# Attention: another order on a shared PSUM bank, and bulk transfers in parts that wait for a group's maxima

## The chip, the cores and the metric

One NeuronCore of a Trainium2 chip runs the whole kernel in one launch. Its engines work from their own instruction streams and meet at semaphores: TensorE (PE; its weight loads are shown as PEld), VectorE (DVE), ScalarE (ACT), GpSimd (POOL) and SyncE (SP), which here only issues DMA transfers. All transfers run on the core's 16 DMA engines; SyncE's show as queue q1, ScalarE's as q10. The metric is the device time of the kernel in microseconds (us).

## The reference

x has 8 sequences of 512 tokens with 128 channels. Four layers add to it, each on a layer norm of x: an RWKV recurrence, a mixture of experts, the attention of this case, and the same mixture of experts again. The attention, cut to what matters (16 heads of 8 channels):

```
q, k, v   = x @ Wq, x @ Wk, x @ Wv                    # split into heads
amp(t)    = softplus(t) / sqrt(mean(softplus(t)**2, over the head) + 1e-6)
q_phi     = pi * tanh(x @ Wqp);   k_phi = pi * tanh(x @ Wkp)
scores    = (q.k + lam * (amp(q) cos(q_phi) . amp(k) cos(k_phi)
                        + amp(q) sin(q_phi) . amp(k) sin(k_phi))) / sqrt(8)
out       = softmax(causal(scores)) @ v               # over the keys, 512
x         = x + out @ Wo
```

So a query and a key of a head are vectors of 24 numbers, and the score is one dot product. The softmax is taken with the row's maximum subtracted.

## The kernel before, in words

`attention_stage` (L704) works on 8 **blocks** b, one sequence each. A block has two **units** q of 8 heads, and a unit two halves of 4 heads. I call a half a **quarter** of the block: quarter g = 0 to 3 is unit g // 2, half g % 2. A quarter is ten **slots**; the block's slots are numbered 0 to 39 here. All engines walk the same slots in program order, each at its own pace.

What TensorE does in a slot: `scores` (L1009) computes a piece of the scores of the current unit into one of three regions (`attn_ps_q`, `attn_ps_v`), which ScalarE exponentiates (L1205 to L1210); `scores_for_maximum` (L961, L966, L970) computes scores of the *next* unit the other way round into three further regions (`attn_ps_p`, `attn_ps_t`), of which VectorE takes row maxima (L1458); and `between` does what the slot has besides. `weigh_values` (L1034) multiplies the exponentials of the quarter before with the values, in slots 3 and 5 of a quarter.

**Maxima.** For each quarter the maxima are transposed into the shared bank by TensorE (`turn_maxima`, L996), copied negated by ScalarE (`take_maxima`, L1225), the remainder is split off by VectorE (`split_maxima`, L1463, with the semaphore step at L1466), and ScalarE sends both parts by two transfers of 8 KB (`send_maxima`, L1230) into two rows of the stack of queries, so that the matmul subtracts them. TensorE may not start the quarter's first `scores` before they have landed (`neg_max_landed`). M0a, M0b, M1a, M1b name these uses for unit 0 or 1 and half a or b. M1a is turned in the first half of quarter 1 for the quarter that follows, M0b in quarter 0, M1b in quarter 2, and M0a of the next block in quarter 3.

**The shared bank.** `attn_ps_f` is one PSUM bank that eight kinds of work use in turn: M0a to M1b as above; A0 and A1, the means of the squared softplus of queries and of keys of block b + 2 (`mean`, L942; ScalarE's `log_of_mean`, L1180, frees the bank); E0 and E1, the outputs of a unit turned (`turn_output`, L1044; VectorE's `normalise`, L1476 and L1478, frees it); FT, the normalised rows turned (L1050; ScalarE's L1235 frees it); FW, the projection (`project`, L1056; VectorE adds it to x at L1486). The list `order` gives the sequence of uses; every user waits on `f_free` until all uses before its own are through.

**Features.** The amplitudes and circles of block b + 2 are worked out inside block b: `features` says in which slot which step runs, on ScalarE (`size`, `exponential_of_size`, `log_of_sum`, `squares`, `log_of_mean`, `inverse`, `high`) and on VectorE (`softplus`, `amplitude`, `scale_circle`, `low`). Side 0 is the queries, side 1 the keys; `high` and `low` (L1195, L1447) split each of three parts into two numbers for the matmul. ScalarE's `high` of part 1 or 2 waits for VectorE's `scale_circle` of the same.

**SyncE.** Its stream per block: `keep` (L846) writes a side's six parts to DRAM (1536 KB), `refill` (L852 to L856, four transfers, 1152 KB) reads the stack of one quarter of block b + 1 back in the layout for the matmul, once the last scores of that quarter of block b are done, and `fetch` (L842) reads the values of block b + 3 (1792 KB). SyncE issues in program order: what waits holds back all behind it.

## Time and profile before

| | us |
|---|---|
| median of 3 runs (lowest, highest) | 1274.72 (1273.44, 1281.04) |
| the profiled execution's own time | 1278.36 |
| its span | 1276.6 |
| mean granted clock of TensorE | 0.923 |
| attention loop, first to last `scores` | 611.1 to 1033.7 |

The quarter starts in the trace (the first L1009 matmul of each) are, for blocks 1 to 6: 671.0, 683.7, 699.5, 716.0; 728.4, 742.1, 755.5, 771.3; 785.7, 799.6, 813.0, 828.8; 841.7, 855.1, 868.5, 884.3; 896.6, 908.1, 920.8, 936.8; 950.2, 962.8, 974.9, 986.6. A row of the view by windows gives for each engine the busy time and the number of instructions inside, then the granted TensorE clock as a share of 2.4 GHz (0.50 is 1.2 GHz), the busy share of the 16 DMA engines and what they moved. In the view of waits a line says which instruction of an engine stood idle and which instruction or landing ended it. In the timeline the brackets hold the idle time just before. An operation in float32 takes TensorE two instructions or more, which the timeline merges (x2, x4).

### The profile page before, as it was taken

Reading aid. Unit: us, or ns where it says so; the run is one execution under the profiler, and the core shown is the slowest. Engines: PE = TensorE matmul, PEld = TensorE weight load, DVE = VectorE, ACT = ScalarE, POOL = GpSimd, SP = SyncE. Lnnn points to the kernel's source line nnn. Section 1 sums busy time; section 2 is a strip of 40 time slices with the busy share of each in tenths; the row PEclk is TensorE's granted clock in tenths of the full one; section 3 lists DMA queues with packets and bytes.
Section 4 is the critical chain, followed back from the end, with each engine's and each line's share of the span. In section 5 each row is a group of like instructions: output and inputs, shape, how many; then the busy total and the mean of one; then the engine's idle time right before and its main releaser. Section 6 shows DMA issues by size and latency. Waiting matters only on the chain. (4 is left out here: it accounts for less than half of the span.)

```text
span 1276.6 us, 16117 instructions
## 1 busy us (share of the span) xinstructions
PE 1093.0 (86%) x5200; PEld 649.7 (51%) x5200; DVE 906.5 (71%) x1927; ACT 656.6 (51%) x1204; POOL 267.2 (21%) x300
## 2 busy tenths in 40 slices
PE   3888889975999999776788888888888969999996
PEld 1223223324676667434455555555556636666774
DVE  2778998976877876874676666667766618787775
ACT  1234444425555555584556565665755546555553
POOL 1445565630000000220212111121212210000000
PEclk9789998977999999886698898989989989999999
DMA  5000000001232121439776767586755312323311
GB/s 192 0 1 1 0 0 1 0 1 46 88 119 81 67 71 63 102 129 259 248 183 141 204 165 193 137 205 169 170 141 136 61 67 67 134 67 99 101 67 66
DMA packets 45502, 129.04 MB, mean 101 GB/s; under 512 B 6512, under 2 KB 8560, under 8 KB 38768
## 3 DMA queue, kind: packets, MB, share of 16 engines
q1 hardware_dynamic: 43376, 127.53, 35.4%
q8 instruction: 41, 0.67, 0.2%
q10 hardware_dynamic: 2048, 0.53, 0.2%
q14 instruction: 37, 0.30, 0.1%
HBM read 88.72 MB, written 36.70 MB: 98 GB/s over the span
## 5 line engine op out<-in xcount | busy, mean ns | idle before, releaser
L1458 DVE TENSOR_REDUCE attn_maxima<-attn_ps_p 128x1 f32<-128x512 f32 (+3 forms) x235 | 146.0, 637 | 106.0 <-PE attn_ps_p L966 88.2
L1377 POOL TENSOR_SCALAR_AFFINE_SELECT attn_probs<-attn_probs 128x512 f32<-128x512 f32 x128 | 84.7, 696 | 321.8 <-ACT attn_probs L1210 321.8
L1835 ACT ACTIVATE moe_hidden<-moe_ps_h 128x512 f32<-128x512 f32 x128 | 76.3, 596 | 146.0 <-PE moe_ps_y L1773 144.3
L961 PE MATMUL attn_ps_p<-attn_stack 96*128 96x384 f32 (+3 forms) x341 | 121.3, 399 | 11.0 <-DVE attn_maxima L1458 10.0
L1957 DVE TENSOR_TENSOR moe_gated<-moe_ps_y,moe_gate_all 128x512 f32<-128x512 f32 x106 | 73.1, 690 | 75.2 <-issue 46.8
L1009 PE MATMUL attn_ps_q<-attn_stack 128*128 128x128 f32 (+3 forms) x343 | 108.8, 381 | 12.4 <-DMA attn_stack<-attn_neg_max 10.9
L1755 PE MATMUL moe_ps_h<-moe_x_high,moe_w_high 128*128 128x512 f32 x256 | 107.4, 420 | 0.0
L1458 DVE TENSOR_REDUCE attn_maxima<-attn_ps_t 128x1 f32<-128x384 f32 (+3 forms) x117 | 74.4, 636 | 44.1 <-PE attn_ps_t L966 41.8
L1757 PE MATMUL moe_ps_h<-moe_x_high,moe_w_low 128*128 128x512 f32 x256 | 102.8, 402 | 0.0
L1756 PE MATMUL moe_ps_h<-moe_x_low,moe_w_high 128*128 128x512 f32 x256 | 102.4, 400 | 0.0
L1771 PE MATMUL moe_ps_y<-moe_hidden_high,moe_w_low 128*128 128x512 f32 x128 | 101.0, 789 | 0.0
L587 POOL TENSOR_TENSOR rwkv_rs<-rwkv_recept,rwkv_state 128x512 f32<-128x512 f32 x64 | 75.9, 1186 | 104.9 <-DVE rwkv_state L668 102.3
L668 DVE TENSOR_TENSOR_SCAN rwkv_state<-rwkv_decay,rwkv_kv 128x512 f32<-128x512 f32 x64 | 91.5, 1429 | 3.2
L1988 DVE TENSOR_TENSOR moe_hidden_low<-moe_hidden,moe_hidden_high 128x512 fp32r<-128x512 f32 x128 | 87.6, 685 | 6.3 <-ACT moe_hidden_high L1836 6.2
L1034 PE MATMUL attn_ps_o<-attn_probs,attn_v_ones 128*32 128x512 f32 (+3 forms) x1024 | 87.2, 461 | 1.7 <-POOL attn_probs L1377 1.7
L224 POOL TENSOR_TENSOR moe_rstd<-moe_var_eps,minus_half 128x4 f32<-128x4 f32 x16 | 16.1, 1009 | 313.0 <-DVE moe_var_eps L208 313.0
L961 PEld LDWEIGHTS attn_ps_p<-attn_stack 96*128 96x128 f32 x341 | 68.8, 215 | 22.4 <-DVE attn_maxima L1458 17.5
L1009 PEld LDWEIGHTS attn_ps_q<-attn_stack 128*128 128x128 f32 x343 | 60.6, 201 | 36.0 <-issue 16.9
L1838 ACT ACTIVATE moe_hidden<-moe_ps_h 128x512 f32<-128x512 f32 x128 | 77.1, 602 | 0.4 <-PE moe_ps_h L1757 0.4
L1966 DVE TENSOR_TENSOR moe_total<-moe_total,moe_gated 128x512 f32<-128x512 f32 x112 | 76.4, 682 | 0.3
L1836 ACT ACTIVATE moe_hidden_high<-moe_ps_h 128x512 fp32r<-128x512 f32 x128 | 75.7, 591 | 0.0
L1207 ACT ACTIVATE attn_probs<-attn_ps_q 128x512 f32<-128x512 f32 x86 | 51.7, 601 | 32.8 <-PE attn_ps_q L1009 29.9
(256 smaller groups left out, 2426.8 us busy)
## 6 DMA issues: line engine op xcount, KB each, us to landing
moe_gate_all<-moe_gates SPq DMA_DIRECT2D x128, 256.0 KB, 4.9
attn_kept<-attn_parts SPq DMA_DIRECT2D x16, 1536.0 KB, 7.9
attn_stack<-attn_kept SPq DMA_DIRECT2D x64, 384.0 KB
attn_stack<-attn_kept SPq DMA_DIRECT2D x64, 192.0 KB
attn_value<-attn_values SPq DMA_DIRECT2D x5, 1792.0 KB, 12.3
attn_values<-attn_early SPq DMA_DIRECT2D x2, 1792.0 KB, 5.7
attn_values<-attn_probs SPq DMA_DIRECT2D x2, 1792.0 KB, 21.9
experts_in_w<-in_w SPq DMA_DIRECT2D x2, 1024.0 KB, 11.3
```

The costliest lines, as they stand in the source:

```text
L668: nc.vector.tensor_tensor_scan(state[:, n, 1:T + 1], decay[:, s, :], kv[:, n % 2, :], 0.0, ALU.mult, ALU.add).then_inc(state_ready, 1)
L961: return mm(tiles(m)[:, i, :], stack[0][q][0:ROWS, h + i, t * P:(t + 1) * P], stack[1][q][0:ROWS, h + i, 0:(t + 1) * P], **flags)
L1009: return mm(ps_h[n % 3][:, at:at + width], stack[1][q][:, h, j * P:(j + 1) * P], stack[0][q][:, h, j * P:T], start=True, stop=True)
L1034: last = mm(ps_o[32 * hh:32 * hh + 32, j * P:T], v_ones[:, b % 2, j, 4 * g + hh, :], probs[:, g % 2, hh, at:at + width], start=(g % 2 == 0 ...
L1377: nc.gpsimd.affine_select(out=tile, in_=tile, compare_op=ALU.is_ge, fill=0.0, base=0, pattern=[[0, 4], [1, P]], channel_multiplier=-1).the ...
L1458: nc.vector.tensor_reduce(maxima[:, u % 2, h:h + heads, t], tiles, AX_X, ALU.max).then_inc(g_free, 1)
L1755: mm(out[:], w1_high[:, cols], x_high[:, c % 3, :], start=True, stop=False)
L1756: mm(out[:], w1_high[:, cols], x_low[:, c % 3, :], start=False, stop=False)
L1757: mm(out[:], w1_low[:, cols], x_high[:, c % 3, :], start=False, stop=True).then_inc(up_done, 1)
L1771: mm(ps_y[s][:], w2_low[:, first], hidden_high[:, s, :], start=False, stop=False)
L1838: fn(hidden[:, s, T:], ps_h[s][1][:], ACT.Gelu).then_inc(gelu_done, 1)
L1988: tt(hidden_low[:, s, :], hidden[:, s, 0:T], hidden_high[:, s, :].bitcast(F32), ALU.subtract).then_inc(low_ready, 1)
```

## The change

Three things are changed, all inside `attention_stage`; the arithmetic is the same.

1. **The order on the shared bank.** A0 of block b + 2 moves from behind FT and FW to between M0b and E1: TensorE does it in slot 5 instead of slot 20. E0 goes from slot 28 to 29, FW from slot 17 to 18, the splits of maxima from the fifth to the fourth slot of a quarter, the normalisation of E0 from slot 29 to 30, the residual add from 18 to 19.
2. **The features' slots.** The first steps of side 0 (`size` to `softplus`) run in the last eight slots of the block before (for block 2, ahead of the loop), the others of side 0 about 15 slots earlier, and each `high` at least three slots behind its `scale_circle`.
3. **SyncE.** Each `keep` becomes two of 768 KB (the high parts, the low parts), `fetch` becomes one of 768 and one of 1024 KB. `sent(u, half)` waits until the maxima of that quarter have landed; one stands ahead of each later part. In a block: refill 0, fetch part 1, *wait for M1a*, fetch part 2, refill 1, keep of side 0 high, *wait for M1b*, keep low, refill 2, *wait for M0a*, keep of side 1 high, refill 3, keep low, *wait for M0b*.

```diff
-    STACK = 4 * 16
+    STACK, KEPT = 4 * 16, 2 * 16
...
         order += [("M0b", b)]
+        order += [("A0", b + 2)] if b + 2 < NB else []
         order += [("E1", b - 1)] if b else []
         order += [("M1a", b)]
         order += [("FT", b - 1), ("FW", b - 1)] if b else []
-        order += [("A0", b + 2)] if b + 2 < NB else []
         order += [("M1b", b)]
...
-            def fetch(b):
-                sp.wait_ge(stored[b], 16)
-                for s in range(2):
-                    sp.wait_ge(low_ready[s], 3 * (b - 1))
-                sp.wait_ge(v_ready, b - 1)
-                sp.dma_start(value[b % 2][:].rearrange("p n t -> p (n t)"), value_kept[b]).then_inc(loaded[b % 2], 16)
...
+            def fetch(b, part):
+                if part == 0:
+                    sp.wait_ge(stored[b], 16)
+                    for s in range(2):
+                        sp.wait_ge(low_ready[s], 3 * (b - 1))
+                    sp.wait_ge(v_ready, b - 1)
+                at = slice(0, 3 * T) if part == 0 else slice(3 * T, FULL)
+                sp.dma_start(value[b % 2][:].rearrange("p n t -> p (n t)")[:, at],
+                             value_kept[b][:, at]).then_inc(loaded[b % 2], 16)
+
+            def keep(b, s, part):
+                if part == 0:
+                    sp.wait_ge(high_ready[s], 3 * b + 3)
+                else:
+                    sp.wait_ge(low_ready[s], 3 * b + 3)
+                at = slice(3 * part, 3 * part + 3)
+                sp.dma_start(scratch[b][s].rearrange("n d h t -> (d h) n t")[:, at, :],
+                             parts[s][:, at, :].bitcast(F32)).then_inc(kept[s], 16)
+
+            def sent(u, half):
+                sp.wait_ge(neg_max_landed[half], (u + 1) * 32)
...
+            for b in range(LAST):
+                keep(b + 1, 1, 1)
+                sent(2 * b, 1)
+                refill(b, 0, 0)
                 if b + 3 < NB:
-                    fetch(b + 3)
-                if b < LAST:
-                    refill(b, 1, 0)
+                    fetch(b + 3, 0)
+                sent(2 * b + 1, 0)
+                if b + 3 < NB:
+                    fetch(b + 3, 1)
+                refill(b, 0, 1)
                 if b + 2 < NB:
-                    keep(b + 2, 0)
-                if b < LAST:
-                    refill(b, 1, 1)
+                    keep(b + 2, 0, 0)
+                sent(2 * b + 1, 1)
+                if b + 2 < NB:
+                    keep(b + 2, 0, 1)
+                refill(b, 1, 0)
+                sent(2 * b + 2, 0)
+                if b + 2 < NB:
+                    keep(b + 2, 1, 0)
+                refill(b, 1, 1)
...
-                if g == 2 and at == 0 and b + 2 < NB:
+                if g == 0 and at == 5 and b + 2 < NB:
                     mean("A0", b + 2)
...
-                if at == 8 and g == 2:
+                if at == 9 and g == 2:
                     turn_output("E0", b)
```

A few lines of ScalarE's `features` and `between`:

```diff
+                if k == 6:
+                    log_of_mean(b, 0)
...
                 if k == 14:
-                    high(b, 0, 0)
+                    high(b, 0, 1)
...
-                if k == 21:
-                    log_of_mean(b, 0)
...
-                if k == 25:
-                    high(b, 0, 1)
...
                     features(b + 2, 20 * q + k)
+                if b + 3 < NB:
+                    features(b + 3, 20 * q + k - 40)
```

And of VectorE's:

```diff
+                if k == 11:
+                    scale_circle(b, 0, 1)
...
-                if k == 25:
-                    scale_circle(b, 0, 1)
...
-                if at == 4:
+                if at == 3:
...
-                if at == 9 and g == 2:
+                if at == 0 and g == 3:
                     normalise("E0", b)
```

How the instructions stand in three places. The changed kernel's line numbers are 11 to 25 higher for the same function. **TensorE in slots 5 to 7 of a block**, before and now:

```order
L1034 MATMUL attn_ps_o<-attn_probs,attn_v_ones 32x256 x4
L1034 MATMUL attn_ps_o<-attn_probs,attn_v_ones 32x128 x4
L1009 MATMUL attn_ps_v<-attn_stack 128x384
L1009 MATMUL attn_ps_v<-attn_stack 128x128
L961 MATMUL attn_ps_t<-attn_stack 128x512
```

```order
L1055 MATMUL attn_ps_o<-attn_probs,attn_v_ones 32x256 x4
L1055 MATMUL attn_ps_o<-attn_probs,attn_v_ones 32x128 x4
L963 MATMUL attn_ps_f<-attn_soft,attention_in_mean_head 128x512
L1030 MATMUL attn_ps_v<-attn_stack 128x384
L1030 MATMUL attn_ps_v<-attn_stack 128x128
L982 MATMUL attn_ps_t<-attn_stack 128x512
```

A0's matmul (L963) has come in behind the weighing of slot 5, three slots ahead of E1. **VectorE at the end of quarter 0 and in quarter 1**, before and now:

```order
L1478 TENSOR_TENSOR attn_xn<-attn_ps_f,attention_in_w 128x4x64
L1427 SCALAR_TENSOR_TENSOR attn_amp<-attn_value,attn_soft 128x512
L1458 TENSOR_REDUCE attn_maxima<-attn_ps_p 128x4
L1458 TENSOR_REDUCE attn_maxima<-attn_ps_t 128x2
L1458 TENSOR_REDUCE attn_maxima<-attn_ps_p 128x2
L1458 TENSOR_REDUCE attn_maxima<-attn_ps_p 128x1
L1427 SCALAR_TENSOR_TENSOR attn_amp<-attn_value,attn_soft 128x512
L1458 TENSOR_REDUCE attn_maxima<-attn_ps_t 128x1
L1463 SCALAR_TENSOR_TENSOR attn_neg_max<-attn_ps_f,attn_neg_max 16x128
```

```order
L1503 TENSOR_TENSOR attn_xn<-attn_ps_f,attention_in_w 128x4x64
L1483 TENSOR_REDUCE attn_maxima<-attn_ps_p 128x4
L1458 SCALAR_TENSOR_TENSOR attn_amp<-attn_amp,attention_in_columns,attn_soft 128x512
L1483 TENSOR_REDUCE attn_maxima<-attn_ps_t 128x2
L1468 TENSOR_TENSOR attn_value<-attn_value,attn_amp 128x512
L1483 TENSOR_REDUCE attn_maxima<-attn_ps_p 128x2
L1468 TENSOR_TENSOR attn_value<-attn_value,attn_amp 128x512
L1483 TENSOR_REDUCE attn_maxima<-attn_ps_p 128x1
L1488 SCALAR_TENSOR_TENSOR attn_neg_max<-attn_ps_f,attn_neg_max 16x128
L1472 TENSOR_TENSOR attn_parts<-attn_value,attn_parts 128x512
L1483 TENSOR_REDUCE attn_maxima<-attn_ps_t 128x1
```

The two softplus have left; the amplitude (L1458 of the changed kernel), both scalings (L1468) and the low part (L1472) of the queries stand between the reductions of quarter 1's first slots, and the split has one reduction fewer ahead of it. **SyncE from the fetch on**, before and now:

```order
L842 DMA attn_value<-attn_values 128x3584 [waits attn_low_ready1,attn_v_ready,attn_low_ready0,attn_stored3]
L852 DMA attn_stack<-attn_kept 48x2048 [waits attn_h_done]
L853 DMA attn_stack<-attn_kept 24x2048
L855 DMA attn_stack<-attn_kept 24x2048
L856 DMA attn_stack<-attn_kept 48x2048
L846 DMA attn_kept<-attn_parts 128x6x512 [waits attn_low_ready0]
```

```order
L844 DMA attn_value<-attn_values 128x1536 [waits attn_low_ready1,attn_v_ready,attn_low_ready0,attn_stored3]
L844 DMA attn_value<-attn_values 128x2048 [waits attn_neg_max_landed0]
L863 DMA attn_stack<-attn_kept 48x2048 [waits attn_h_done]
L864 DMA attn_stack<-attn_kept 24x2048
L866 DMA attn_stack<-attn_kept 24x2048
L867 DMA attn_stack<-attn_kept 48x2048
L853 DMA attn_kept<-attn_parts 128x3x512 [waits attn_high_ready0]
L853 DMA attn_kept<-attn_parts 128x3x512 [waits attn_low_ready0,attn_neg_max_landed1]
```

The fetch now stands one refill earlier in the block (behind refill 0 instead of refill 1), and its second part and the keep's second part wait for a landing of maxima.

## Rows read from the trace of the kernel before

**Rows 1.** Windows (blocks 4, 6, loop): window, length, busy per engine, PEclk, DMA share, GB/s

```profile
841.70:896.60 54.90, 47.32 (x336) 30.36 (x336) 36.76 (x67) 32.94 (x65) 11.12 (x18) 0.95 0.70 177
950.20:996.50 46.30, 42.54 (x335) 27.57 (x335) 29.91 (x55) 25.92 (x50) 10.71 (x18) 1.00 0.63 138
611.10:1033.70 422.60, 363.64 (x2573) 232.45 (x2573) 275.49 (x494) 250.21 (x486) 91.91 (x146) 0.93 0.63 159
```

**Rows 2.** Windows of single quarters; in order of the text: blocks 1, 4, 5

```profile
683.70:699.50 15.80, 14.37 (x91) 9.66 (x91) 7.52 (x14) 8.81 (x18) 3.12 (x6) 0.78 0.39 77
841.70:855.10 13.40, 12.87 (x81) 8.71 (x82) 6.46 (x11) 6.80 (x14) 2.48 (x4) 0.78 0.73 192
855.10:868.50 13.40, 11.66 (x93) 7.66 (x93) 9.03 (x17) 10.26 (x22) 3.53 (x6) 1.00 0.48 91
868.50:884.30 15.80, 12.40 (x89) 7.56 (x89) 9.87 (x18) 8.13 (x17) 2.39 (x4) 1.00 0.71 192
884.30:896.60 12.30, 10.39 (x81) 6.44 (x80) 11.40 (x22) 7.74 (x16) 2.72 (x4) 1.00 0.88 236
896.60:908.10 11.50, 10.50 (x82) 6.74 (x82) 7.51 (x14) 7.75 (x16) 2.85 (x4) 1.00 0.86 232
936.80:950.20 13.40, 12.78 (x81) 8.31 (x78) 10.90 (x20) 6.52 (x14) 2.84 (x4) 0.76 0.77 208
```

**Rows 3.** Waits of TensorE, 625 to 1045: us in total, times, longest

```profile
PE attn_ps_q L1009 <- DMA attn_stack<-attn_neg_max: 9.7, 6, 2.9
PE attn_ps_f L1044 <- ACT attn_soft L1180: 7.5, 6, 1.3
PE attn_ps_f L942 <- DVEq L1466: 5.6, 6, 0.9
PE attn_ps_f L1044 <- ACT attn_o_rows L1218: 4.6, 9, 0.7
PE attn_ps_f L1056 <- ACT attention_in_w L1235: 4.3, 8, 0.7
PE attn_ps_f L1050 <- DVEq L1466: 4.3, 7, 0.8
PE attn_ps_v L1009 <- DMA attn_stack<-attn_neg_max: 3.4, 3, 1.8
PE attn_ps_f L942 <- DVE x_rows L1486: 1.8, 5, 0.4
```

**Rows 4.** Timeline, block 4's third quarter: start, us, engine, what, idle before it

```profile
877.88 1.46 ACTq L1230 DMA_DIRECT2D attn_stack<-attn_neg_max  x2
...
878.06 1.10 PE L942 MATMUL attn_ps_f<-attn_soft,attention_in_mean_head 128*128 128x512 f32 x2 [0.93 <-DVEq L1466]
...
880.96 0.63 ACT L1195 ACTIVATE attn_parts<-attn_value 128x512 fp32r<-128x512 f32 x1 [4.17 <-DVE attn_value L1443]
...
882.45 0.69 ACT L1180 ACTIVATE attn_soft<-attn_ps_f,attention_in_columns 128x512 f32<-128x512 f32 x1
...
883.29 0.63 PE L1044 MATMUL attn_ps_f<-identity,attn_o_rows 128*128 128x128 f32 x4 [1.26 <-ACT attn_soft L1180]
```

**Rows 5.** Tile attn_neg_max, issue to landing: sent in 862.5:867, 877.5:882.5, 778.5:786

```profile
DMA to landing us min/median/max: 2.2/2.3/2.3
...
DMA to landing us min/median/max: 3.2/3.3/3.4
...
DMA to landing us min/median/max: 3.9/4.8/5.6
```

**Rows 6.** Windows around the maxima sent at 877.88; columns as in rows 1

```profile
877.00:880.00 3.00, 2.07 (x16) 1.30 (x10) 1.08 (x4) 0.00 (x0) 0.00 (x0) 1.00 0.92 388
880.00:881.00 1.00, 1.00 (x7) 0.60 (x5) 1.00 (x3) 0.04 (x1) 0.00 (x0) 1.00 0.11 29
```

**Rows 7.** VectorE by form, 671 to 950: busy us, mean ns, idle before

```profile
L1447 DVE TENSOR_TENSOR attn_parts<-attn_value,attn_parts 128x512 fp32r<-128x512 f32 x30 | 23.4, 779 | 0.0
L1443 DVE TENSOR_TENSOR attn_value<-attn_value,attn_amp 128x512 f32<-128x512 f32 x20 | 13.6, 681 | 0.0
```

More of the change, by code:

```diff
@@ L825, in wait_loaded @@
         def wait_loaded(engine, b):
-            engine.wait_ge(loaded[b % 2], (b - 1) // 2 * 16)
+            engine.wait_ge(loaded[b % 2], (b - 1) // 2 * 32)
         block = ctx.enter_context(nc.Block())
@@ L870, in _ @@
             store(4)
-            keep(0, 0)
-            keep(0, 1)
+            for s in range(2):
+                for part in range(2):
+                    keep(0, s, part)
             sp.wait_ge(zeroed, 32)
             for s in range(2):
-                sp.wait_ge(kept[s], 16)
+                sp.wait_ge(kept[s], KEPT)
             stack_heads(0, 0, 0)
@@ L883, in _ @@
             store(7)
-            keep(1, 0)
-            for b in range(NB):
-                if b < LAST:
-                    keep(b + 1, 1)
-                    refill(b, 0, 0)
-                    refill(b, 0, 1)
-                if b + 3 < NB:
-                    fetch(b + 3)
-                if b < LAST:
-                    refill(b, 1, 0)
-                if b + 2 < NB:
-                    keep(b + 2, 0)
-                if b < LAST:
-                    refill(b, 1, 1)
+            keep(1, 0, 0)
+            keep(1, 0, 1)
+            keep(1, 1, 0)
+            for b in range(LAST):
+                keep(b + 1, 1, 1)
+                sent(2 * b, 1)
+                refill(b, 0, 0)
+                if b + 3 < NB:
+                    fetch(b + 3, 0)
[3 more added lines that the diff above has]
+                refill(b, 0, 1)
+                if b + 2 < NB:
+                    keep(b + 2, 0, 0)
[7 more added lines that the diff above has]
+                refill(b, 1, 1)
         @block.tensor
@@ L1237, in features @@
             def features(b, k):
-                if k == 4:
+                if k == -7:
                     size(b, 0)
-                if k == 5:
+                if k == -6:
                     exponential_of_size(b, 0)
+                if k == -4:
+                    log_of_sum(b, 0)
+                if k == 0:
+                    squares(b, 0)
+                if k == 6:
+                    log_of_mean(b, 0)
                 if k == 7:
-                    log_of_sum(b, 0)
+                    inverse(b, 0)
                 if k == 8:
@@ L1267, in features @@
                     inverse(b, 1)
[L1268 to L1270 removed]
+                if k == 34:
                     high(b, 1, 1)
[L1272 removed]
+                if k == 36:
                     high(b, 1, 2)
@@ L1347, in _ @@
                 inverse(1, s)
+            for k in range(-8, 0):
+                features(2, k)
             for b in (5, 6):
@@ L1488, in features @@
             def features(b, k):
[L1489 removed]
+                if k == -3:
                     softplus(b, 0)
+                if k == 10:
+                    amplitude(b, 0)
+                if k == 11:
+                    scale_circle(b, 0, 1)
+                if k == 12:
+                    scale_circle(b, 0, 2)
                 if k == 13:
+                    low(b, 0, 0)
+                if k == 15:
                     softplus(b, 1)
                 if k == 16:
[L1494 to L1495 removed]
+                    low(b, 0, 1)
+                if k == 18:
+                    low(b, 0, 2)
+                if k == 22:
                     low(b, 1, 0)
[L1497 to L1504 removed]
+                if k == 30:
+                    amplitude(b, 1)
                 if k == 31:
[L1506 removed]
+                    scale_circle(b, 1, 1)
                 if k == 32:
[L1508 to L1511 removed]
                     scale_circle(b, 1, 2)
[L1513 removed]
+                if k == 36:
                     low(b, 1, 1)
[L1515 removed]
+                if k == 38:
                     low(b, 1, 2)
@@ L1529, in between @@
                         split_maxima("M0a", b + 1, 2 * b + 2)
-                if g == 1 and at == 8 and b:
+                if g == 1 and at == 9 and b:
                     add_output(b - 1)
@@ L1537, in between @@
                     features(b + 2, 20 * q + k)
+                if b + 3 < NB:
+                    features(b + 3, 20 * q + k - 40)
                 if b == 0 and q == 0 and k in (2, 3):
@@ L1582, in _ @@
                 scale_circle(1, s, 2)
+            for k in range(-8, 0):
+                features(2, k)
             for b in range(NB):
```

41 lines of the change are left out of this document (9 added, 32 removed).

## The prediction, made before the changed kernel was run

> **What bounds the kernel now.** I read the views in this order: the stretches of the attention loop, the waits of TensorE inside it, the timeline around the largest of them, and then the landings of the small transfers against the load of the DMA engines. The loop is the only place the diff touches; it takes 422.6 us of the 1276.6 us span [rows 1].
>
> TensorE is the bound, but not at its peak. A block with features in it (blocks 0 to 5) takes 54.9 us with TensorE busy for 47.3; block 6, which has the same scores and outputs but no features, takes 46.3 at a full clock [rows 1]. The quarters of one block are very unequal [rows 2]: in block 4 they are 13.4, 13.4, 15.8 and 12.3 us. Two things stretch them. The third quarter (868.5) is busy for only 12.4 of its 15.8 us. And the first quarter of block 4 (841.7; those of blocks 2 and 3 are like it) is busy for 12.9 us where block 5's (896.6), the same work at a granted clock of 1.00, is busy for 10.5: the granted clock averages 0.78 in it, a mixture of 2.4 and 1.2 GHz.
>
> The waits of TensorE name the causes [rows 3]. From 625 us on it waits 9.7 + 3.4 = 13.1 us for the landing of a quarter's negated maxima, and 7.5 + 5.6 + 4.6 + 4.3 + 4.3 = 26.3 us for the shared bank (attn_ps_f). The timeline of block 4's third quarter [rows 4] shows what is behind the largest: ScalarE waits 4.17 us for the scaled circle it must copy (`high` in slot 25, `scale_circle` in the same slot on VectorE), so its logarithm of A1 comes at 882.45, and TensorE, at slot 28, waits 1.26 us for it before E0. Before A1 it had waited 0.93 us for VectorE's split of M1b.
>
> The landings: sent onto quiet DMA engines the maxima need 2.3 us in the median; sent onto busy ones 3.3 and 4.8 us [rows 5]. The 3.3 are of the pair sent at 877.9: the engines are 0.92 busy with 388 GB/s of bulk until 880, and 0.11 in the microsecond after [rows 6].
>
> **The change, part by part.** No arithmetic is added. TensorE, ScalarE and VectorE run the same instructions in another order; SP issues two keeps and one fetch per block more.
>
> 1. *Maxima against bulk.* Today a refill and, behind it, a whole keep (1536 KB) or fetch (1792 KB) are issued at once at the end of a quarter, in three quarters of four, and are still draining when the maxima are sent six or more slots in. The change leaves behind each refill at most one part of 768 KB; the next part goes out when the maxima have landed. In block 4's third quarter the bulk drains at 880, 11.5 us in; a fetch of 1792 KB at 388 GB/s [rows 6] is 4.6 us of that, a part of 768 KB would be 2.0, so the engines would be free 2.6 us earlier, about 9 us in. The maxima leave 9.4 us into it, at 877.88 [rows 4]. Bounds: nothing of the 13.1 us, or all. Two things stop short of all: the fourth bulk burst (refill, half a keep, and the half keep issued late in the quarter before) still ends near the send of M0b, and block 0's is behind the start-up stores. I take 9 us.
>
> 2. *The shared bank.* A0 leaves the crowded stretch after FW for slot 5, between M0b and E1. E0 moves from slot 28 to 29, FW from 17 to 18, all splits one slot earlier, and ScalarE's copies of the circle come three slots or more behind their scaling. A slot is 1.34 us (13.4 us over ten). E0 behind A1 (7.5 us): the 4.17 us wait of ScalarE is gone, E0 is a slot later; 6.5 go. A1 behind the split (5.6): 0.93 each time, less than the slot won; 5 go. FT behind the split (4.3): 3.5 go. FW behind ScalarE's copy (4.3): 4 go. E1 behind the copied output (4.6, with E0's own): here the change adds. ScalarE copies the output in slot 6 and then takes A0's logarithm (0.69 us, [rows 4]) before E1 in slot 8 may write; TensorE has the mean's own matmul, 1.10 us [rows 4], more to do meanwhile; A0 has a wait for a split too. I add 2 us over six blocks. A0's old wait behind the residual add was 1.8; 1.5 go. Sum: 6.5 + 5 + 3.5 + 4 + 1.5 - 2 = 18.5 us. Bounds: nothing, and 26.3 + 1.8 = 28.
>
> 3. *The clock.* Five quarters are at 0.75 to 0.78; three stand in rows 2. Against their like at 1.00 these are busy for 2.4 us more (12.87, against 10.50), 2.7 more (14.37 against 11.66) and 2.4 more (12.78 against 10.39); with the two others like the first, some 12.5 us. Four begin with a landing wait, the fifth follows a wait before E0 like the one in rows 4. Block 6, with a landing wait of its own, stays at 1.00 throughout [rows 1]: the trace shows a coincidence, not the cause. Bounds 0 and 13; I take 9.
>
> 4. *What is late next.* VectorE. Its second quarter is 9.03 us busy of 13.4; its fourth 11.40 of 12.3 [rows 2]. The change puts into the second quarter an amplitude and two scalings (0.68 each, by the scaling) and two low parts (0.78 each) more than it had [rows 7], 3.6 us: 12.6 busy, where the quarter, 13.4 less its two bank waits of 0.8 and 0.5 [rows 3], should last 12.1. The fourth loses one low part and gains a softplus and the normalisation of E0, about 0.7 us: 12.1 in a quarter that without the landing wait behind it should be 11.4. The first and third are light, and TensorE may be three score tiles ahead, so most of this is carried over; not covered it would cost 0.5 + 0.7 = 1.2 us a block. I take that whole, 7 us for six blocks. Before the loop ScalarE has three more activations for block 2, which were inside it, each about as long as the 0.69 us one of [rows 4]: 2 us at the start if nothing hides them; I add 1.5. SP's three more issues stand beside everything. Its new waits hold back the refills behind them, but a refill may go only at the end of a quarter, when these maxima have landed anyway (TensorE itself waits for them there).
>
> Sum: 9 + 18.5 + 9 - 8.5 = 28 us. The profiled execution took 1278.4 us and would take 1250; it lies 3.7 above the median of the runs, 1274.7, and in their range. From the median: **1247 us**.
>
> **A rule that speaks against part 1.** In the trace the loaded maxima land about when the bulk ahead is through: the pair sent at 877.9 lands a microsecond later than a quiet one, at about 881.5, when the engines have just emptied [rows 5, 6]. The Trainium skill, page "DMA: Bandwidth & Descriptors", section "Queues, rings and completion order", says that each engine takes turns between the queues that have work, a packet at a time; then a small transfer on ScalarE's own queue would wait for one packet of bulk, however much stands behind it, and holding parts back would win little. What the trace shows of the loaded landings (4.8 against 2.3 us) speaks for a longer wait than one packet's, but it holds few cases.
>
> **Rivals.**
> - *Landings as late as before* (0.15): lateness comes from any bulk in flight, not from its amount. Parts 1 and 3 give nothing: 18.5 - 8.5 = 10 us, 1265. By the Trainium skill's rule above it would end here. For it: the engines are 0.86 and 0.88 busy over the quarters at 896.6 and 884.3 [rows 2], and a shorter quarter packs the same bytes tighter (0.70 of 54.9 us in block 4 is 38 us of bulk, 0.80 of a block of 48). Against it: the landing follows the drain in rows 6.
> - *VectorE becomes the bound* (0.12): quarters two and four last what VectorE has to do plus a hand-over of one operation each, 0.7 us: 13.3 and 12.8. That is 1.4 us a block more than I took: 1255.
> - *All of it works* (0.10): 13 + 26 + 13 us less 7: 1230.
> - *Slower* (0.04): the new place of A0 becomes what slot 20 to 28 was. ScalarE has in slots 5 to 9 the issue of two transfers, the output, the logarithm, the inverse, a size and a high part beside five exponentials. If it falls over three slots behind there, E1 stalls for the 1.26 + 0.93 us that E0 and A1 stall today, M1a is sent late and its landing costs up to 2.9 us, and the slower clock another 2.7: 7.8 us a block, 47 in six, against the forecast's gain of 28: 1294. It decides once E1's wait passes about 1 us in every block.
> - *No effect* (0.02): the waits only change their names, 1273.
> - The forecast (0.57) spans 1237 to 1257.
>
> **Range and chances.** 1232 to 1265 takes in the forecast, VectorE's bound and half of the first rival; out are about 0.07 below and 0.12 above. One per cent, about what a measurement of this kernel tells from none, is 12.7 us, so faster is below 1262: the forecast, the good case, VectorE's, and a third of the first rival, 0.84. Within 1%: 0.12. Slower: 0.04.
>
> **What the new profile would show.** Part 1: landings near 2.5 us in all quarters, TensorE's wait for them under 4 us in all. Part 2: the third quarters near 12 us, no wait of ScalarE for the scaling, E1's wait under 1 us. Part 3: granted clock 1.00 in most quarters from block 1 on. Part 4: VectorE busy over 11.5 us in the second and fourth quarters, TensorE's waits for reductions up by some 5 us. The whole loop near 394 us. I am wrong if landings stay at 4 us, if the first quarter takes over the stall of the third, or if the second quarter grows over 13.4 us.

## The result, and the profile after

The changed kernel takes 1257.51 us in the median of four runs (1256.41 to 1258.44), beside runs of the kernel before with a median of 1275.9: a ratio of 0.984, 95% interval 0.981 to 0.987. Forecast were 1247 in a range of 1232 to 1265, so the sign and the range hold, and about 10 us of the gain of 28 are missing. One disturbed run of 1980 us, of R7 below, is left out of its ratio.

The whole gain is in the attention loop, 422.6 us before [rows 1]. Windows of the changed kernel, columns as in rows 1: the loop, then the four quarters of block 4.

```profile
613.20:1015.60 402.40, 361.22 (x2575) 233.66 (x2573) 283.48 (x496) 252.59 (x488) 93.90 (x146) 0.93 0.70 167
...
831.90:846.30 14.40, 13.07 (x85) 8.09 (x85) 8.54 (x16) 7.86 (x16) 2.68 (x4) 0.88 0.78 194
846.30:858.00 11.70, 11.13 (x91) 7.63 (x91) 10.85 (x20) 9.12 (x19) 4.00 (x6) 1.00 0.77 172
858.00:871.80 13.80, 11.59 (x85) 7.25 (x85) 10.10 (x17) 8.05 (x16) 4.02 (x6) 1.00 0.84 220
871.80:885.20 13.40, 13.02 (x78) 8.38 (x79) 8.60 (x16) 7.81 (x16) 1.22 (x3) 0.75 0.71 153
```

The loop is 20.2 us shorter, the span 19.9. The second and third quarters have lost 1.7 and 2.0 us against those at 855.1 and 868.5 [rows 2], but the third does not reach the 12 that I forecast, and the first and fourth have each grown by about 1 us. TensorE is busy for 2.4 us less than before, at the same mean clock. The loss is seen in its waits, of the changed kernel from 625 to 1030 (us in total, times, longest):

```profile
PE attn_ps_q L1030 <- DMA attn_stack<-attn_neg_max: 14.5, 12, 2.9
PE attn_ps_p L982 <- DVE attn_maxima L1483: 6.0, 12, 0.8
PE attn_ps_v L1030 <- DMA attn_stack<-attn_neg_max: 5.8, 5, 1.5
...
PE attn_ps_t L982 <- DVE attn_maxima L1483: 4.2, 7, 0.8
PE attn_ps_v L1030 <- DVE attn_maxima L1483: 2.1, 1, 2.1
...
PE attn_ps_f L1017 <- DVE attn_xn L1503: 1.2, 4, 0.3
PE attn_ps_f L1017 <- DVE x_rows L1511: 1.1, 1, 1.1
PE attn_ps_f L1071 <- DVE attn_xn L1503: 0.9, 1, 0.9
PE attn_ps_f L1065 <- ACT attn_o_rows L1239: 0.7, 1, 0.7
PE attn_ps_f L1077 <- ACT attention_in_w L1256: 0.7, 1, 0.7
```

Those for the shared bank (attn_ps_f) are down to 4.6 us, where the six of [rows 3] alone were 28.1. Those for the landing of the maxima, which the parts were to shorten, are up from 13.1 us [rows 3] to 20.3. The landings themselves are slower. Tile attn_neg_max, issue to landing, sends from 640 to 1000, first of the kernel before, then of the changed one:

```profile
DMA to landing us min/median/max: 1.8/2.9/5.6
```

```profile
DMA to landing us min/median/max: 1.8/4.3/7.4
```

The timeline of the changed kernel around one of the late ones, at the start of block 3's fourth quarter, shows how (start, duration, engine, what, idle before it). SPq is SyncE's issue, ACTq ScalarE's:

```profile
811.50 1.16 ACTq L1251 DMA_DIRECT2D attn_stack<-attn_neg_max  x2
...
819.49 0.38 SPq L853 DMA_DIRECT2D attn_kept<-attn_parts  x1
...
819.52 0.50 PE L1030 MATMUL attn_ps_q<-attn_stack 128*128 128x512 f32 x1 [2.93 <-DMA attn_stack<-attn_neg_max]
...
819.91 0.48 SPq L863 DMA_DIRECT2D attn_stack<-attn_kept  x1
```

The pair sent at 811.50 lands after 7.1 us in the median, and TensorE has waited 2.93 us for it. Just before that matmul the keep that `sent` held back goes out, 0.42 us ahead of the refill of the new quarter. Nothing was moved out of the way of the next maxima: the part that should have gone out late in the old quarter goes out first in the new one. The amounts agree: around the start of block 3's third quarter SyncE issues the fetch's second part, a refill and half a keep (1024 + 1152 + 768 KB), ahead of the same maxima for which the kernel before had a refill and a whole fetch (1152 + 1792 KB), 2944 KB both times. SyncE's waits in the changed kernel, 625 to 1016, put a size to it:

```profile
SPq L853 <- DMA attn_stack<-attn_neg_max: 80.3, 12, 12.7
...
SPq L844 <- DMA attn_stack<-attn_neg_max: 40.5, 5, 11.0
```

That is 121 us in which it stood before a keep or a fetch until maxima had landed, 7 us each time, half a quarter.

### The profile page after: what moved, and what is told of

The parts are those of the page before. It is cut to its first block and busy times, and to the rows that moved or that the text cites. A ratio compares the mean times of both kernels' runs of the same rounds, so it can differ in the third digit from the quotient of the medians.

```text
span 1256.7 us, 16161 instructions
## 1 busy us (share of the span) xinstructions
PE 1094.3 (87%) x5200; PEld 654.1 (52%) x5200; DVE 913.6 (73%) x1927; ACT 658.0 (52%) x1204; POOL 269.2 (21%) x300
## 3 DMA queue, kind: packets, MB, share of 16 engines
q1 hardware_dynamic: 44352, 127.53, 37.1%
q10 hardware_dynamic: 2048, 0.53, 0.2%
## 5 line engine op out<-in xcount | busy, mean ns | idle before, releaser
L982 PEld LDWEIGHTS attn_ps_p<-attn_stack 96*128 96x128 f32 x341 | 68.8, 215 | 20.3 <-DVE attn_maxima L1483 13.3
```

The costliest lines, as they stand in the source:

```text
L982: return mm(tiles(m)[:, i, :], stack[0][q][0:ROWS, h + i, t * P:(t + 1) * P], stack[1][q][0:ROWS, h + i, 0:(t + 1) * P], **flags)
```

## The experiments

The runs are R0 to R10 and R12. In R1 and R2 the bank's order and the features stay or go together; R9 takes the one-slot moves alone. Each ratio is to runs of the kernel before on the same chip: R1 to R4 ran together, so did R0, R5, R6 and R7, so did R8, R9 and R10.

**R1, the order alone**: the changed order and features, the whole keeps and fetches of before at their old places, no `sent`.

```diff
-                keep(b + 1, 1, 1)
-                sent(2 * b, 1)
                 refill(b, 0, 0)
-                if b + 3 < NB:
-                    fetch(b + 3, 0)
...
+                    fetch(b + 3)
+                refill(b, 1, 0)
+                if b + 2 < NB:
+                    keep(b + 2, 0)
```

> The changed order on the shared bank and of the features, with SyncE's transfers as before: whole keeps and fetches, no wait for a landing. Theory S (the order is the whole gain, SyncE's part gives nothing because its waits end only at the quarter's end, where the held part then starts together with the next refill): 1254 to 1260 us, landing waits of TensorE 15 to 25 us as in the changed kernel. Rival P (the held parts do shield the maxima, and without them the waits would be longer still, since a shorter quarter packs the bulk tighter): 1263 to 1272, landing waits over 28 us.

**R2, SyncE's part alone**: the order and features of before, SyncE as changed.

```diff
-                if g == 0 and at == 5 and b + 2 < NB:
+                if g == 2 and at == 0 and b + 2 < NB:
                     mean("A0", b + 2)
...
-                if at == 9 and g == 2:
+                if at == 8 and g == 2:
                     turn_output("E0", b)
```

> The order before, with SyncE's parts and waits of the change. Theory S: 1272 to 1279 us, no change, landing waits still 10 to 15 us. Rival P: 1260 to 1268, landing waits under 6 us.

**R3, parts without waits**: the changed kernel with all four calls of `sent` taken out.

```diff
-                sent(2 * b + 1, 0)
                 if b + 3 < NB:
                     fetch(b + 3, 1)
```

> The changed kernel without SyncE's waits for landed maxima; the parts stay split and in their order. Theory S: within 3 us of the changed kernel's 1257.5, since the waits end where the next refill is due anyway. Rival P: 1262 or more, landing waits over 26 us (20 in the changed kernel).

**R4, nothing behind a refill**: every part is put behind the wait for a landing.

```diff
-                keep(b + 1, 1, 1)
                 sent(2 * b, 1)
+                keep(b + 1, 1, 1)
                 refill(b, 0, 0)
-                if b + 3 < NB:
-                    fetch(b + 3, 0)
                 sent(2 * b + 1, 0)
                 if b + 3 < NB:
+                    fetch(b + 3, 0)
                     fetch(b + 3, 1)
```

> The changed kernel with all keep and fetch parts moved behind the landing of their quarter's maxima, so that nothing but the refill stands between a quarter's start and its maxima. Theory D (a landing is late by the bulk still in the queue when it is sent, so the amount ahead decides): landing waits down from 20 to under 10 us, 1240 to 1250 us. Rival R (any bulk in flight delays it alike, a packet at a time): landing waits 15 to 20, 1255 to 1260. Rival L (the deferred parts start at the quarter's end all the same and meet the next refill): 1255 or more, landings still 5 us and more.

| | median us | ratio (95%) | loop us | waits for landings |
|---|---|---|---|---|
| R1 order alone | 1250.16 | 0.978 (0.974 to 0.982) | 402.4 | 16.7 |
| R2 SyncE alone | 1307.03 | 1.022 (1.018 to 1.027) | 450.3 | 32.3 |
| R3 parts, no waits | 1245.18 | 0.972 (0.969 to 0.976) | 394.3 | 15.8 |
| R4 all behind landings | 1272.23 | 0.994 (0.991 to 0.996) | 420.5 | 35.7 |

(The last column sums the two rows in which `scores` waits for attn_neg_max, of one profiled execution each; R0 below, the changed kernel again, has 23.2 where the first execution has 20.3.) The order and the features carry the whole gain. On SyncE's side the waits cost: with them 0.984, without them 0.972, and the more is put behind them, the worse. Of what I expected, rival P failed in each. Theory S, which put SyncE's part at nothing, failed too: R1 came out 4 us below its range, R2 28 us above it, and R3 is 1.2% faster than the changed kernel where S allowed 3 us. R4's time is rival L's. R1's profiled execution was its slowest (1264.75, where its lowest is 1247.65), so its loop overstates it; by the medians the order alone is also better than the order with the change's SyncE, though the two intervals just overlap. Whether parts without waits are better than none stays open: the intervals of R1 and R3 overlap.

**R0, the changed kernel once more**, beside the next three.

> The changed kernel itself, so that the runs beside it can be set against it on one chip: ratio 0.981 to 0.988 to the kernel before.

It repeats: 1259.57, ratio 0.984 (0.981 to 0.988).

**R5, the wait ends at the split**: `sent` waits for VectorE's split of the same maxima instead of their landing.

```diff
             def sent(u, half):
-                sp.wait_ge(neg_max_landed[half], (u + 1) * 32)
+                sp.wait_ge(neg_low, 2 * u + half + 1)
```

> The changed kernel with each of SyncE's waits ending when VectorE has split the maxima, so just before ScalarE sends them, instead of when they have landed. Theory C (a wait for the landing carries the held part over the quarter's end, ahead of the next refill, and so makes the next landing late in its turn): the held parts now go in the quarter they belong to, landing waits down from 20 to 10 to 15 us, ratio 0.970 to 0.976, as without waits or better. Rival H (what costs is any wait of SyncE at all, since it holds its queue up): ratio 0.980 to 0.988, as the changed kernel.

Measured 1242.0, ratio 0.970 (0.965 to 0.975), loop 389.1, landing waits 12.6: theory C's numbers. Holding parts back costs nothing that shows beside R3; holding them until the landing does. Timeline of R5 around the same quarter's start, block 3's fourth:

```profile
798.16 0.38 SPq L853 DMA_DIRECT2D attn_kept<-attn_parts  x1
798.17 1.16 ACTq L1251 DMA_DIRECT2D attn_stack<-attn_neg_max  x2
...
802.26 0.32 SPq L863 DMA_DIRECT2D attn_stack<-attn_kept  x1
...
803.58 0.51 PE L1030 MATMUL attn_ps_q<-attn_stack 128*128 128x512 f32 x1 [0.34 <-DMA attn_stack<-attn_neg_max]
```

The keep leaves with the maxima, 4 us before the refill, not in front of it, and TensorE waits 0.34 us where it waited 2.93.

**R6, all parts behind the split**: R4's places with R5's wait.

> All keep and fetch parts behind the split of their quarter's maxima, so that only the refill is ahead of a send. Theory D (bulk that stands in the queue when the maxima are sent delays them, bulk issued afterwards doesn't): landing waits under 8 us, ratio 0.960 to 0.970. Rival R (any bulk in flight delays them alike, also what comes behind): landing waits 15 us and more, ratio 0.972 to 0.985.

Measured 1245.41, ratio 0.973 (0.970 to 0.977), loop 384.5, landing waits 15.4, where the same places with the wait for the landing gave 0.994 and 35.7 (R4). These are rival R's numbers, but the run did not put the bulk behind the maxima, as the rows show. Two sends of R6 stand next to each other, one beside bulk and one in the clear. Its timeline, then issue to landing of the two pairs, then windows around them:

```profile
799.44 0.92 SPq L853 DMA_DIRECT2D attn_kept<-attn_parts  x2
799.45 1.16 ACTq L1249 DMA_DIRECT2D attn_stack<-attn_neg_max  x2
...
805.59 0.51 PE L1028 MATMUL attn_ps_q<-attn_stack 128*128 128x512 f32 x1 [1.07 <-DMA attn_stack<-attn_neg_max]
...
812.30 0.51 ACTq L1249 DMA_DIRECT2D attn_stack<-attn_neg_max  x1
```

```profile
DMA to landing us min/median/max: 4.7/5.1/5.6
...
DMA to landing us min/median/max: 1.8/1.8/1.9
```

```profile
797.00:799.40 2.40, 2.40 (x27) 1.15 (x23) 1.29 (x3) 0.98 (x2) 0.00 (x0) 1.00 0.81 133
800.00:803.00 3.00, 3.00 (x15) 1.94 (x16) 1.57 (x4) 1.73 (x4) 0.00 (x0) 1.00 0.92 326
803.00:806.00 3.00, 1.93 (x13) 1.24 (x13) 2.15 (x4) 1.90 (x4) 1.03 (x2) 1.00 1.13 327
811.50:814.50 3.00, 3.00 (x29) 1.96 (x28) 2.30 (x5) 2.85 (x6) 0.00 (x0) 1.00 0.04 8
```

The first pair needs 3.3 us more than the one in the clear. It was not ahead of the bulk. SyncE and ScalarE wait for the same split; the first part's issue starts 0.005 us before the send, here and in all 17 such pairs of the loop, the second part's 0.12 us before the second transfer's, and until 799.40 the engines were 0.81 busy with the refill.

**R7, nearly no bulk**: R3 with the keeps (from block 2) and the fetches cut to 16 columns, and refills that read the stack of block 1. It bounds what landings and their traffic cost.

```diff
-                at = slice(0, 3 * T) if part == 0 else slice(3 * T, FULL)
+                at = slice(0, 16) if part == 0 else slice(3 * T, 3 * T + 16)
...
-                stack_heads(b + 1, q, half)
+                stack_heads(1, q, half)
```

> Without SyncE's waits, and with the keeps from block 2 on and the fetches cut to 16 columns of each part; the refills stay whole and read block 1's stack. It leaves out work: the attention of later blocks is not the reference's. It prices the keeps' and fetches' contention. Theory D and C both: landing waits under 5 us, VectorE's tiles the only large wait left, ratio 0.955 to 0.965. If the slower clock follows the landing waits, the loop's time at half clock falls from 58 us to under 35; if it has other causes it stays over 45 and the ratio is 0.962 to 0.972.

Measured 1228.06, ratio 0.960 (0.955 to 0.964). The loop of R7, as a window, and its landings (sends from 620 to 980):

```profile
608.00:977.90 369.90, 344.20 (x2573) 223.02 (x2573) 283.46 (x495) 251.25 (x487) 95.09 (x146) 0.97 0.55 107
```

```profile
DMA to landing us min/median/max: 1.8/2.1/4.4
```

The waits for landings are under 1 us in all, and reductions are the only large wait left, as expected. Against R3 the loop loses 24.4 us, of which 12.2 are TensorE's busy time: the granted clock goes from 0.94 there (0.93 in the changed kernel) to 0.97, and the time at half clock from 58 us in the changed kernel to about 21.

**R8, the old order with parts and no waits**: R2 without `sent`.

> The order before, with SyncE's parts but without its waits for landings. Theory C (the waits do the harm, the split as such none): within 1% of the kernel before, ratio 0.990 to 1.005, where the same with waits was 1.022. Rival K (more and smaller transfers harm by themselves, or the old order cannot bear the parts' places, since a keep part that waits for a late low part holds up the refill behind it): ratio 1.012 or more.

Measured 1308.57, ratio 1.023 (1.019 to 1.027): the same as R2 and rival K's number. Here I was wrong: I had put R2's loss down to the waits, and they add nothing. The timeline of R8, from the start of a quarter (843.1) to the start of the next, and SyncE's largest waits, 625 to 1060:

```profile
843.89 5.36 SPq L853 DMA_DIRECT2D attn_kept<-attn_parts  x2
...
849.29 0.48 SPq L860 DMA_DIRECT2D attn_stack<-attn_kept  x1
...
854.18 1.15 ACTq L1244 DMA_DIRECT2D attn_stack<-attn_neg_max  x2
...
861.39 0.80 PE L1023 MATMUL attn_ps_q<-attn_stack 128*128 128x512 f32 x1 [3.92 <-DMA attn_stack<-attn_neg_max]
```

```profile
SPq L853 <- ACT attn_parts L1209: 125.6, 12, 17.1
...
SPq L860 <- PE attn_ps_q L1023: 56.6, 8, 11.4
...
SPq L853 <- DVE attn_parts L1461: 20.1, 6, 4.6
```

Both parts of the queries' keep now stand ahead of this refill. The first waits for ScalarE's last `high` (slot 29 in the old features) until 843.89, which costs little, as the refill may go only from 843.1 on. The second waits 4.6 us more for VectorE's last `low` (slot 31, in the next quarter). So the refill goes out at 849.29, about 5 us after it could, and is still under way when the maxima leave at 854.18. The pair needs 6.4 us, and TensorE waits 3.92. R3 has the same places with the new order and the features 15 slots earlier, and 0.972. So R2 and R8 price this clash with the old features; they say nothing of what the parts alone would do.

**R9, five moves of one slot**: the kernel before, with FW and E0 on TensorE a slot later, the splits a slot earlier, and the residual add and E0's normalisation a slot later. This is the whole edit beside the one line `if at == 4` that becomes `if at == 3`:

```diff
-                if g == 1 and at == 7 and b:
+                if g == 1 and at == 8 and b:
                     project(b - 1)
-                if at == 8 and g == 2:
+                if at == 9 and g == 2:
                     turn_output("E0", b)
...
-                if g == 1 and at == 8 and b:
+                if g == 1 and at == 9 and b:
                     add_output(b - 1)
-                if at == 9 and g == 2:
+                if at == 0 and g == 3:
                     normalise("E0", b)
```

> The kernel before with the one-slot moves alone: splits a slot earlier, E0 and its normalisation, FW and the residual add a slot later; A0, the features and SyncE as before. Theory M (the bank's waits are mostly a slot short each): bank waits of TensorE down from 29 to under 16 us, ratio 0.985 to 0.992. Rival F (the features' places cause them, by ScalarE's 4 us wait for the scaled circle): bank waits still over 20 us, ratio 0.992 to 1.003; A0, now one slot closer behind the residual add, waits longer.

Measured 1242.24, ratio 0.972 (0.969 to 0.976), loop 386.6: with A0, the features and SyncE left alone, it is faster than the changed kernel. It is no slower than R1 either (0.978, the intervals just overlap), which has these moves and those of A0 and the features: nothing shows that the latter two gain anything. Of R9: the loop and the four quarters of a block as windows, TensorE's waits for the bank from 625 to 1020, and the wait of ScalarE that I had blamed:

```profile
610.10:996.70 386.60, 348.66 (x2573) 225.96 (x2573) 276.15 (x494) 248.32 (x486) 91.75 (x146) 0.96 0.70 174
817.70:830.50 12.80, 10.50 (x86) 6.72 (x83) 9.88 (x20) 9.74 (x20) 3.52 (x6) 1.00 0.82 217
830.50:841.50 11.00, 11.00 (x90) 7.61 (x90) 7.40 (x13) 8.23 (x17) 2.92 (x6) 1.00 0.61 113
841.50:856.30 14.80, 12.70 (x89) 7.66 (x87) 10.69 (x19) 7.78 (x16) 2.39 (x4) 1.00 0.81 211
856.30:868.20 11.90, 10.07 (x80) 6.40 (x78) 10.68 (x21) 8.34 (x17) 3.31 (x5) 1.00 0.93 236
```

```profile
PE attn_ps_f L942 <- DVE x_rows L1486: 4.7, 5, 1.0
...
PE attn_ps_f L1044 <- ACT attn_soft L1180: 1.7, 6, 0.3
```

```profile
ACT attn_parts L1195 <- DVE attn_value L1443: 25.3, 10, 3.2
```

E0's wait falls from 7.5 [rows 3] to 1.7, and those for the split, 5.6 and 4.3, are gone, though ScalarE still waits up to 3.2 us for the scaled circle. All bank waits together are 13.3 us, under theory M's 16, where they were 31.7; only A0 behind the residual add is up, from 1.8 to 4.7, as rival F said. The time is well below both ranges. Of the loop's 36.0 us, 18.4 are bank waits, 2.9 landing waits, and 15.0 TensorE's busy time (363.64 to 348.66, at 0.96 for 0.93), which I had not forecast for these moves and whose cause is open.

**R10, maxima sent a slot earlier** (R5 with `send_maxima` in a quarter's slot 4 instead of 5), to give the landing more time.

```diff
-                if at == 5:
+                if at == 4:
                     if g == 0:
                         send_maxima(2 * b, 1)
```

> As the version whose SyncE waits end at the split, with ScalarE sending the maxima one slot earlier, right behind the split. If landing waits are a matter of when the maxima leave: down from 13 to 7 us or less, ratio 0.962 to 0.968. If an earlier send only meets more of the refill, or ScalarE now waits for VectorE's split: landing waits the same within 2 us, ratio 0.968 to 0.976.

Measured 1256.85, ratio 0.982 (0.978 to 0.986): what R5 had won is lost again, and the waits for landings are 15.6 us, 3 more than R5's. ScalarE's sends stand in its own stream and wait for the split; its exponentials queue behind them. TensorE's waits for exponentials, R10 from 613 to 1020:

```profile
PE attn_ps_q L1030 <- ACT attn_probs L1226: 8.7, 13, 1.5
PE attn_ps_v L1030 <- ACT attn_probs L1226: 4.3, 6, 1.1
PE attn_ps_q L1030 <- ACT attn_probs L1228: 1.6, 2, 1.5
```

14.6 us, against 3.6 in R5 (4.3 in the changed kernel). ScalarE's own idle time ahead of these exponentials, same window, where R5's is under 1 us:

```profile
ACT attn_probs L1226 <- issue: 21.1, 13, 1.9
```

**R12, ScalarE's circle copies later**: R9 with `high` of parts 1 and 2 of the queries in slots 28 and 30, which takes the wait for the scaling away from the third quarter.

```diff
-                if k == 25:
+                if k == 28:
                     high(b, 0, 1)
...
-                if k == 29:
+                if k == 30:
                     high(b, 0, 2)
```

> The one-slot moves on the kernel before, and ScalarE's two later copies of the queries' circle three slots and one slot later (28 and 30, with VectorE's low parts at 30 and 32), so that ScalarE doesn't wait for the scaling in the third quarter. Theory M2 (that wait is what still holds the third quarter at 14.8 us): third quarters under 13.5 us, ratio 0.960 to 0.968 against 0.972 for the moves alone. Rival (the third quarter is long by its two means and the residual add ahead of A0, not by ScalarE): third quarters still over 14 us, ratio 0.969 to 0.975.

Measured 1248.7, ratio 0.975 (0.972 to 0.979), no better than R9, and the rival's number. The wait for the scaled circle is no longer among ScalarE's waits, and the third quarters of blocks 1 to 5 last 14.0 to 14.9 us, where R9's last 14.8 to 15.0: little of their length was this wait. In both runs A0 stands behind the residual add for 4.7 and 4.8 us; the rest of what makes the third quarter long I did not settle.

## Why the prediction was right or wrong

**The bank: right, mis-sized.** Forecast were 18.5 us of 28.1, E1's new wait of 2 us among them. Of the six rows two are left, 0.7 each, and the wait behind the residual add has gone from A0 to a turn of maxima (1.1, L1017); by all rows on attn_ps_f the waits fall from 31.7 to 4.6, by 27. E1's 2 us did not come: L1065 behind the copied output is 0.7. My caution was misplaced: a stall of 0.7 to 1.3 us that recurs in every block is mostly gone when the two sides move a slot (1.34 us) apart. But one reason was wrong. I credited 6.5 us at E0 to the end of ScalarE's 4.17 us wait for the scaled circle [rows 4] and the slot together; R9 keeps that wait and wins 5.8 there by the slot alone, and R12 removes it for nothing.

**The parts: the step that failed.** It was the sentence that SyncE's "new waits hold back the refills behind them, but a refill may go only at the end of a quarter, when these maxima have landed anyway". Each half is true, and together they defeat the part: since the landing starts the next quarter, a part behind it goes out not within its own quarter, as I costed it, but at the head of the next one, beside or ahead of the refill. Forecast 9 us less, measured 7.2 more (13.1 to 20.3). R3 and R5 show it by taking the wait away (0.972) or ending it at the split (0.970), R4 by putting more behind it (0.994). The wait is not the whole miss, though: R3 and R5 still have 15.8 and 12.6 us of landing waits, near the 13.1 of before, where my sum left 4. I had also assumed that the maxima leave as late as before. In a quarter shortened by the bank's gain they leave 6.4 us in (811.50 in the quarter of 805.1), not 9.4 [rows 4], and find 1448 KB of bulk issued and not yet started. And R1 has 16.7 us without any parts, so some of the rise goes with the order; how much is not shown, as its profiled execution was its slowest.

The rival "landings as late as before" came nearest in that parts and clock gave next to nothing. Its time was 1265; the measured one is lower because the bank gave some 8 us more. Its reason, that any bulk in flight delays and not its amount, is not what the packets show (R6).

**The rule on queues.** If engines took turns a packet at a time, and that were all, a small transfer beside bulk would lose one packet's time. The page of the changed kernel has 44352 packets with 127.53 MB on SyncE's queue, 2.9 KB each; at 326 GB/s over 16 engines one takes about 0.14 us. The pair in R6 lost 3.3 us, and its packets started when nearly all the bulk issued before them had. The Trainium skill, page "DMA: Bandwidth & Descriptors", section "Queues, rings and completion order", states that rule, and that a packet is typically 9 to 17 descriptors. No run here shows that the profile's packets are such packets. If each of the keep's in the trace (2 KB, 0.09 us) were one descriptor, a turn would cost 0.8 to 1.5 us, an estimate from the page's figure. The second transfer's packets started 3.2 us later than in the clear, which is more than one such turn. So the 3.3 us do not agree with the rule as a price of one turn. The packet records name no engine: whether an engine takes longer turns or goes by the order of issue stays open.

**The clock: not gained.** Forecast 9 us, measured 2.4 (busy time 363.64 to 361.22, both at 0.93). I had tied it to the landing waits, and those did not go. In the runs the two go together only loosely: granted 0.90 to 0.91 in R2 and R4 with 32 and 36 us of such waits, 0.93 in the changed kernel with 20, 0.96 in R9 with 10, 0.97 in R7 with under 1. In R7 TensorE is busy for 17.0 us less than in the changed kernel. But R6, with 15.4 us of them, is at 0.97 too, and R3, with 15.8, at 0.94:

```profile
609.50:994.00 384.50, 346.64 (x2573) 223.11 (x2573) 282.78 (x496) 251.37 (x488) 95.62 (x146) 0.97 0.72 175
```

So the sum of these waits does not decide the clock, and what does stays open.

**VectorE: over-costed.** I forecast 12.6 us busy in the second quarter and 12.1 in the fourth; in block 4 they are 10.85 and 8.60. The steps were counted rightly: seven stand in the second quarter's slots, against two before (of the two softplus only the queries' left, the keys' went from slot 13 to 15). But VectorE runs behind TensorE's quarters, and the work is spread: the first quarter goes from 6.46 [rows 2] to 8.54, the second from 9.03 to 10.85, and the fourth, which I had rising, falls from 11.40 to 8.60. TensorE's waits for reductions rise from 9.6 (6.5 and 3.1 in the kernel before) to 12.3, where I had put 7 us more. The loop starts at 613.2 instead of 611.1, for which I had added 1.5; R5, with the same code ahead of it, starts at 608.8, so that term was neither confirmed nor refuted.

**The sum.** Bank -27.1, landings +7.2, clock -2.4, reductions +2.7: -19.6 us, and the loop measures -20.2. The sign was right, and two terms were wrong in opposite directions: too much from the parts, too little from the bank. That the time lies in the range by 7 us owes much to luck: with 18.5 from the bank and the rest as measured it would have been about 1264 by my estimate, at its edge. It is luck too that R3's loop, 394.3, is the forecast's 394: its landing waits are 15.8 us and not 4.

**The versions to keep.** R5 (0.970), R9 (0.972), R3 (0.972), R6 (0.973) and R12 (0.975) have the lowest ratios of those that do the whole work, and their intervals overlap. R9 is the smallest edit by far. R9's slots together with R5's parts were not run.

## What to carry to other kernels

A wait that holds back background transfers must end before the point at which the next urgent batch is due. If it ends on the very event that starts the next phase, it turns late work into early work for that phase. If it ends on the event that also releases the urgent transfer, see which of the two is issued first: here the bulk was, by 0.005 us. In an issue queue that works in order, nothing whose producer is late may stand ahead of what is due. And when a stall recurs at about a microsecond per turn, first move its two sides one slot apart: here five such moves (0.972) gave more than the whole change (0.984), though only half of what they gave was bank waits.

## What the runs showed of the hardware

- Two transfers of 8 KB land in 1.8 us on idle DMA engines (R6, at 812.30). With a part of a keep issued on another queue 0.005 us before the first and another between the two they took 4.7 to 5.6; with 1448 KB of refill and keep or fetch ahead of them 6.8 to 7.4 (changed kernel, 811.50). Their packets started when nearly all the bulk issued before them, on the other queue, had started.
- The same 2573 matmul instructions kept TensorE busy for 344.2 us at a granted clock of 0.97 (R7) and for 371.8 at 0.91. The second row is R2's loop:

```profile
612.70:1063.00 450.30, 371.80 (x2573) 238.49 (x2573) 275.39 (x495) 250.27 (x487) 91.60 (x146) 0.91 0.63 149
```

What lowered the clock in R2, and whether the late transfers did, is not shown.
